# Two-layer graph network on one core: border tiles of the second stage summed once, into a window of 128 nodes that spans two blocks

## The reference

```python
e   = relu(ea @ ee_w1 + ee_b1) @ ee_w2 + ee_b2
agg = segment_sum(x[src] + e, dst, num_segments=n)
h   = (1.0 + eps) * x + agg
h   = relu(_ln(h @ w1 + b1, g1, be1))      # 256 -> 1024
h   = relu(_ln(h @ w2 + b2, g2, be2))      # 1024 -> 1024
out = relu(_ln(x + h @ w3 + b3, bn_g, bn_b))
```

## Time and profile before

| | |
|---|---|
| median of 3 runs | 1556.49 us (1520.37, 1556.49, 1563.42) |
| the profiled execution | 1535.62 us, span 1533.7 us |
| mean granted clock of TensorE | 0.874 of full |
| PE busy | 1254.0 us, 82% of the span |
| DVE busy | 959.9 us, 63% |
| POOL busy | 824.7 us, 54% |
| ACT busy | 678.4 us, 44% |

### The profile page before, as it was taken

One profiled execution on the slowest core, in us unless ns is written; L12 is line 12 of the kernel. 1 busy time (PEld: TensorE's weight loads), 2 busy tenths in 40 slices (PEclk: granted clock), 3 DMA queues, 4 the chain that ended last, 5 costly groups with the idle time before them and its releaser, 6 DMA issues.

```text
span 1533.7 us, 21066 instructions
## 1 busy us (share of the span) xinstructions
PE 1254.0 (82%) x5295; PEld 993.8 (65%) x5295; DVE 959.9 (63%) x2787; ACT 678.4 (44%) x1654; POOL 824.7 (54%) x840
## 2 busy tenths in 40 slices
PE   4888878888879978877877878886888788878997
PEld 3666666666667666766655756665667667656776
DVE  4766666776666776766744655554565556546665
ACT  2455555565555664545332423332443334323443
POOL 6656555666556666654654564443555456544530
PEclk9788889998878989889988988888898889979999
DMA  6435445555455444546654564544555556554530
GB/s 194 114 112 154 140 134 154 159 155 157 141 146 145 133 134 129 157 126 184 186 153 127 154 189 129 148 141 121 158 154 160 153 145 178 156 149 136 161 111 16
DMA packets 106088, 222.13 MB, mean 145 GB/s; under 512 B 20003, under 2 KB 57369, under 8 KB 106010
## 3 DMA queue, kind: packets, MB, share of 16 engines
q0 software_dynamic: 53408, 164.16, 38.3%
q1 hardware_dynamic: 52602, 57.11, 12.1%
HBM read 203.96 MB, written 17.23 MB: 144 GB/s over the span
## 4 chain that ended last, share of the span: by engine, by line
PE 49%; another core or an unknown queue 15%; issue 14%; DVE 10%; ACT 10%; DMA 1%; POOL 0%; DVEq 0%; ACTq 0%; POOLq 0%; SPq 0%
PE ps_z L1307 21%; PE ps_e L1040 8%; PE ps_y L1307 4%; PE ps_sum L1045 4%; PE ps_sum L1047 4%; PE ps_s L1262 3%; ACT msg L1579 3%; DVE msg L2071 2%; DVE msg L2077 2%; ACT msg L1582 2%; ACT aF L1804 2%; PE ps_tr L1376 2%; DVE oh L159 1%; PE ps_w L1141 1%
## 5 line engine op out<-in xcount | busy, mean ns | idle before, releaser
L963 POOL DMA_INDIRECT grow<-table_dram,src_all x401 | 386.0, 963 | 379.5 <-PE ps_s L1262 250.1
L908 POOL DMA_INDIRECT raw<-in_x,src_all x399 | 404.5, 1014 | 257.4 <-DVE msg L2077 143.7
L1307 PE MATMUL ps_z<-w_high,a 128*128 128x512 f32 x784 | 292.3, 441 | 77.3 <-issue 60.5
L2071 DVE SCALAR_TENSOR_TENSOR msg<-raw,w_sb,msg 128x256 fp32r<-128x256 f32 x416 | 183.8, 482 | 212.2 <-ACT msg L1582 139.0
L1040 PE MATMUL ps_e<-we,attr 65*128 65x256 f32 x832 | 254.9, 431 | 47.2 <-DVE msg L2077 36.6
L1045 PE MATMUL ps_sum<-msg,oh 128*128 128x512 f32 x464 | 251.9, 543 | 29.7 <-DVE msg L2077 23.0
L1307 PEld LDWEIGHTS ps_z<-w_high,a 128*128 128x128 f32 x784 | 167.1, 214 | 130.6 <-issue 78.6
L1582 ACT ACTIVATE msg<-ps_e 128x512 fp32r<-128x512 f32 (+1 forms) x220 | 124.1, 564 | 254.3 <-remote 158.9
L1040 PEld LDWEIGHTS ps_e<-we,attr 65*128 65x128 f32 x832 | 175.2, 217 | 94.7 <-issue 62.0
L159 DVE TENSOR_SCALAR oh<-lane,rel 128x128 fp32r<-128x128 f32 x915 | 209.4, 291 | 3.6 <-issue 3.4
L1047 PE MATMUL ps_sum<-msg,oh 128*128 128x512 f32 x464 | 203.0, 437 | 6.3 <-issue 6.2
(11 more groups left out here) (182 smaller groups left out, 1577.8 us busy)
## 6 DMA issues: line engine op xcount, KB each, us to landing
attr<-in_attrT SPq DMA_DIRECT2D x50, 192.0 KB
raw<-in_x,src_all POOLq DMA_INDIRECT x416
grow<-table_dram,src_all POOLq DMA_INDIRECT x401
w_raw<-in_m_w SPq DMA_DIRECT2D x48, 128.0 KB
table_dram<-table SPq DMA_DIRECT2D x23, 256.0 KB
attr<-in_attrT SPq DMA_DIRECT2D x24, 160.0 KB
xs<-in_x SPq DMA_DIRECT2D x24, 128.0 KB
xTb<-in_xT SPq DMA_DIRECT2D x24, 128.0 KB
```

What stands on the lines that cost most here:

```text
L908: pool.indirect_dma_start(out=raw[:, j, :], out_offset=None, in_=x, in_offset=bass.IndirectOffsetOnAxis(ap=src_all[:, q * TILES + j:q * TI ...
L963: pool.indirect_dma_start(out=grow[:, j, :].bitcast(F32), out_offset=None, in_=table_dram, in_offset=bass.IndirectOffsetOnAxis(ap=src_all[ ...
L1307: mm = pe.matmul(acc, left[a], right[b], start=False, stop=stop and a == 1, skip_group_check=True)
L2071: dve.scalar_tensor_tensor(msg[:, j, 1, 0:D], raw[:, j, :], w_sb[:, tile_cols(n, j)], msg[:, j, 0, 0:D].bitcast(F32), ALU.mult, ALU.subtract)
```

## The change

In the program that the inputs select, positions 3 to 24 no longer run step 0 at all, and no longer tile 0 of step 1. A border's two tiles (tile 16 of a block and tile 0 of the block behind) are summed once: their one-hot matrices are made against 128 nodes that begin at node 64 of this block and end at node 63 of the block behind, the window. Each such tile is two matmuls of 256 columns (high part, low part) into columns 256 to 511 of `ps_y`. ACT writes zeros there first (`open_window`). When the sums of a position are done, DVE adds partitions 64 to 127 of the window to h, a third addition in `take_h`, and in the next pass adds partitions 0 to 63 to `hbx` (`carry`), before that position's h is taken. Position 2 makes the first window, positions 0 and 1 stay as they were. The test at the start now asks of the first and last `edge` tiles of a block that their targets lie within 64 nodes of the border. `sum_done` keeps its values: where step 0 is gone, step 1 adds 2. The numbers in `row_free` are unchanged, so tile 16's buffer still waits for the value 10p + 1, which now comes with step 1.

```diff
+LANES, WINDOW = 1, 2
+WINDOWS = 2
+HALF = P // 2
+def has_window(p):
+    return not isinstance(p, int) or p >= WINDOWS
+def behind_window(p):
+    return not isinstance(p, int) or p > WINDOWS
 class Near:
+    def tile_kind(self, p, c, j):
+        span = self.steps[c][0]
+        if behind_window(p) and (c == 0 or span == 0 and j < self.edge):
+            return None
+        if has_window(p) and (span == 1 or span == 0 and j >= TILES - self.edge):
+            return WINDOW
+        return LANES
     def sum_inc(self, p, c):
...
+        if behind_window(p):
+            return c + 1 if c == self.steps_at(p)[0] else 1
# TensorE
+                def add_window_tile(j, slot):
+                    for half in range(2):
+                        mm = pe.matmul(ps_y[:, D:2 * D], oh[:, slot, :], grow[:, j, half * D:(half + 1) * D],
+                                       start=False, stop=False, skip_group_check=True)
+                    return mm
                 def near_step(path, p, c):
...
                     for j in range(j0, j0 + m):
+                        kind = path.tile_kind(p, c, j)
+                        if kind is None:
+                            continue
+                        if kind == WINDOW and (c, j) == path.first_window(p):
+                            pe.wait_ge(window_open, p - WINDOWS + 1)
                         pe.wait_ge(got[j], 16 * path.fills(p + span, j))
-                        mm = add_tile(j, path.slot[c] + j - j0, c == first and j == j0,
-                                      c == last and j == j0 + m - 1)
+                        if kind == LANES:
+                            mm = add_tile(j, path.slot[c] + j - j0, (c, j) == first, (c, j) == last)
+                        else:
+                            mm = add_window_tile(j, path.slot[c] + j - j0)
# ScalarE
+                def open_window(p):
+                    wait(act, carried, p - WINDOWS)
+                    act.activation(ps_y[:, D:2 * D], lane[:, 0:D], ACT.Copy, scale=0.0).then_inc(window_open, 1)
                     if exists(i - 2):
                         finish_std(i - 2, 1)
+                    if exists(i + 1):
+                        open_window(i + 1)
                     if exists(i - 1):
                         deviation(1, i - 1)
# VectorE
+                def make_window_lanes():
+                    dve.wait_ge(oh2_ready, SUMS)
+                    dve.tensor_copy(lane[:, 0:HALF], lane[:, P:P + HALF]).then_inc(window_lanes, 1)
+                    dve.tensor_copy(lane[:, 3 * P:3 * P + HALF], lane[:, 2 * P:2 * P + HALF])
+                    dve.tensor_copy(lane[:, 3 * P + HALF:4 * P], lane[:, P + HALF:2 * P]).then_inc(window_lanes, 1)
                 def take_h(b, steps, loaded, windows=True):
...
+                    if windows and behind_window(b):
+                        dve.wait_ge(carried, b - WINDOWS)
                     dve.tensor_tensor(h[:, :], ps_s[:, 0:D], hbx[:, :], ALU.add).then_inc(h_half, 1)
...
+                    dve.tensor_tensor(h[:, :], ps_s[:, D:2 * D], h[:, :], ALU.add).then_inc(h_summed, 1)
+                    dve.wait_ge(h_summed, b - WINDOWS + 1)
+                    dve.wait_ge(y_done, b - 1)
+                    dve.tensor_tensor(h[HALF:P, :], ps_y[HALF:P, D:2 * D], h[HALF:P, :], ALU.add)\
+                       .then_inc(h_ready, 1)
+                def carry(b):
+                    dve.wait_ge(hb_in, 16 * (b + 1))
+                    dve.tensor_tensor(hbx[0:HALF, :], ps_y[0:HALF, D:2 * D], hbx[0:HALF, :], ALU.add)\
+                       .then_inc(carried, 1)
                     if exists(i):
                         h_low(i)
+                    if exists(i + 1):
+                        carry(i)
                     if exists(i - 2):
                         finish2(i - 2)
```

More of the change, by code:

```diff
@@ L82, in __init__, with steps_at, tiles, first_and_last @@
         self.ahead = [k for k in range(LAST_PAIRS, NP) if PAIRS[k][0] + PAIRS[k][1] <= TILES - edge]
+    def steps_at(self, p):
+        if not behind_window(p):
+            return sum_steps_at(p)
+        return [c for c in range(1, SUMS) if any(self.tile_kind(p, c, j) for j in self.tiles(c))]
+    def tiles(self, c):
+        _, j0, m = self.steps[c]
+        return range(j0, j0 + m)
+    def tile_kind(self, p, c, j):
[5 more added lines that the diff above has]
+        return LANES
+    def first_and_last(self, p):
+        steps = self.steps_at(p)
+        if isinstance(p, int) and p == 1:
+            steps = self.ahead[0:1] + steps
+        plain = [(c, j) for c in steps for j in self.tiles(c) if self.tile_kind(p, c, j) == LANES]
+        return plain[0], plain[-1]
+    def first_window(self, p):
+        return [(c, j) for c in self.steps_at(p) for j in self.tiles(c) if self.tile_kind(p, c, j) == WINDOW][0]
     def sum_inc(self, p, c):
@@ L89, in sum_inc, with one_hot_inc @@
             return 1 + len(self.ahead)
+        if behind_window(p):
+            return c + 1 if c == self.steps_at(p)[0] else 1
         return sum_inc_at(p, c)
+    def one_hot_inc(self, p, steps):
+        if behind_window(p):
+            return steps[-1] + 1 if steps[0] == self.steps_at(p)[0] else len(steps)
+        return sum(sum_inc_at(p, c) for c in steps)
     def one_hots(self, p, c):
@@ L1282, in near_step @@
                     span, j0, m = path.steps[c]
-                    first, last = sum_steps_at(p)[0], sum_steps_at(p)[-1]
-                    if isinstance(p, int) and p == 1:
-                        first = path.ahead[0]
-                    if c == first:
+                    first, last = path.first_and_last(p)
+                    if c == first[0]:
                         wait(pe, h_ready, p)
@@ L1384, in sums @@
                 def sums(path, p, first, end):
-                    for c in sum_steps_at(p):
+                    for c in path.steps_at(p):
                         if first <= c < end:
@@ L1853, in late_iteration @@
                     h_high(i)
+                    if i + 1 == WINDOWS:
+                        act.wait_ge(w_ready, LAYER_2)
+                        act.wait_ge(window_lanes, 2)
+                        open_window(WINDOWS)
                     deviation(1, i - 1)
@@ L2010, in _ @@
                 lim = TILES - edge
[L2011 to L2013 removed]
+                parts = ((slice(0, edge), -HALF, HALF), (slice(edge, lim), 0, P), (slice(lim, TILES), HALF, P + HALF))
+                for part, low, _ in parts:
+                    ins = dve.tensor_scalar(bad[:, n, :, part], rel[:, :, part], float(low), None, ALU.is_lt)
+                ins.then_inc(prep, 1)
                 dve.wait_ge(prep, 6 + 2 * n)
[L2015 to L2018 removed]
+                for part, _, above in parts:
+                    ins = dve.scalar_tensor_tensor(bad[:, n, :, part], rel[:, :, part], float(above),
+                                                   bad[:, n, :, part], ALU.is_ge, ALU.add)
+                ins.then_inc(prep, 1)
                 dve.wait_ge(prep, 7 + 2 * n)
@@ L2326, in near_oh @@
                 def near_oh(path, p, group):
-                    steps = [c for c in range(OH_GROUPS[group][0], OH_GROUPS[group][1] + 1) if c in sum_steps_at(p)]
+                    steps = [c for c in range(OH_GROUPS[group][0], OH_GROUPS[group][1] + 1) if c in path.steps_at(p)]
                     if not steps:
```

37 lines of the change are left out of this document (22 added, 15 removed).

## The result

| | before | changed |
|---|---|---|
| median, us | 1541.41 (4 runs, 1520.37 to 1563.42) | 1668.49 (4 runs, 1662.30 to 1691.08) |
| ratio, 95% interval | | 1.094 (1.086 to 1.102) |
| span of the profiled execution | 1533.7 | 1660.5 |
| PE busy | 1254.0 | 1253.4 |
| mean granted clock | 0.874 | 0.843 |

The account below looks back on a forecast made before the run. It took each pass as bound by a burst of 17 gathers that slows all engines but POOL, then PE's leftover work. Terms of -5.5 + 0.3, about -5 us, took 1546 to 1541 us; range 1515 to 1566.

Parts of the forecast that it names:

- The gather of tile 16: In POOL's list: released later, it delays tiles 0 to 3 by 0.45 us, already counted; not late for its reader, nothing more.
- The 8.5 us: In the loop: part of an average 31.9 us pass that PE needn't work, measured against a pass of 23.4 us.
- rival 1: Loop passes: the stall pattern shifts favourably, -20 us, with the half-clock price of removed matmuls about 1510 us; chance 0.12.
- PE's net of -9.3 us: On PE, positions 2 to 24: 9.9 us of matmuls removed, less 0.6 us for window tiles, at full clock.
- 2.9 us: On PE: the change's saving by the Trainium skill's matmul spacing, set aside because the trace disagreed.
- take_h: On DVE: two one-hots fewer, one 64-partition addition more, upper bound 425 ns taken; together about zero.
- The carry: On DVE: up to 0.425 us before the second stats, hidden in clean passes; 0 to 1.7 us, taken as 0.
- open_window: On ACT: 0.37 us, 23 times, hidden before an instruction waiting for DVE's stats; 8.5 us at most.
- Rival 2: Loop passes: carry and late release slow it, up to 0.88 us a pass; 1565 us, or 1574 at half clock; chance 0.10.
- Rival 3: Loop's back edge: instruction fetches cost 6.1 us in each of 21 passes, +128 us, about 1670 us; chance 0.02.
- The range: For the whole kernel's time: 1515 to 1566 us, leaving out less than 2 in 10.

Follow-up runs that it names:

- e1: The kernel before, with only the release of tile 16's gather moved from step 0 to step 1; 1663.53 us, 1.088 of the kernel before.
- e2: The changed kernel, with tile 4's gather waiting two steps longer (step 4 instead of step 2); 1483.37 us, 0.968 of the kernel before.
- e17: The changed kernel with short pauses before tiles 4, 10 and 16 of every position, and pauses in the first stage; 1413.83 us, 0.933 of the kernel before.
- e18: The kernel before with the same pauses as e17; 1405.60 us, 0.928 of the kernel before.
- e11: The changed kernel with a short pause before tile 7, and before tiles 6 and 12 in the first stage; 1458.02 us, 0.953 of the kernel before.
- e13: e11 with the carry moved behind layer 2's normalization and open_window behind that layer's first relu; 1438.15 us on another chip.
- e14: The kernel before with the pauses of e11 and a dummy DVE instruction of the carry's size in its place; 1405.44 us on another chip.
- e4: The kernel before with a second pause in each burst, before tile 10 until tile 9's gather has landed; 1472.42 us, 0.954 of the kernel before.

## Why the prediction was wrong

**The failed step** is "The gather of tile 16": "all of them start later with it, as just counted ... Cost nothing more". The shift itself was right: from the first sum to the burst's first gather it is 1.72 us now (899.59 to 901.31) and was 1.16 (1070.21 to 1071.37), 0.56 us where 0.45 was said. But I counted it against PE's sums of this pass only, not against the other thing in POOL's queue that waits for the same semaphore. Relative to the burst, step 2 comes 1.0 us earlier (2.5 us behind the first gather for 3.5). That removes the pause of 1.96 us ahead of tile 4, and with it what had kept the stall to the burst's end. e1 has this and nothing else of the change and loses as much; e2 puts a pause back and wins it all.

The row was there to read. In the pass that I quoted as the clean one, POOL stands for 1.96 us behind its fifth gather, and in the pass of 48.3 us ahead of it it does not:

```profile
1031.92 0.95 POOL L963 DMA_INDIRECT grow<-table_dram,src_all  x1 [9.46 <-PE ps_s L1262]
...
1038.37 0.95 POOL L963 DMA_INDIRECT grow<-table_dram,src_all  x1 [0.51 <-issue]
1039.62 0.95 POOL L963 DMA_INDIRECT grow<-table_dram,src_all  x1 [0.30 <-issue]
1041.93 0.95 POOL L963 DMA_INDIRECT grow<-table_dram,src_all  x1 [1.37 <-remote]
```

That burst rests only behind its seventh gather, for 1.37 us, and PE's first gap comes 9.4 us after its start. The whole loop is like that. Of the 21 passes between the two marks of the earlier trace rows, four last over 35 us (38.4, 42.2, 48.3 and 43.4), and they are the four whose burst has no rest of over 1.5 us; in the other 17 bursts POOL rests 1.7 to 2.1 us behind the fifth gather (once 4.2), and PE's first gap comes 9.3 to 14.3 us after that rest. Each of the four is followed by one of the four passes of 23.4 to 23.5 us. So even the clean pass is not free of a stall: that of its own burst sets in at 1089.8, behind the next mark (1087.93). The 8.5 us by which I set it under the average were read off one half of a pair. I had read only POOL's last and first gather of a burst and took its 17 gathers for a constant, in rival 1 too: "Against: burst length and POOL's list are the same". The list was, the timing within it was not. "In which all engines but POOL slow down near the end" should have been asked further: near the end of what, and in which bursts early?

**PE's net of -9.3 us** was sized by rows that hold: 365 matmuls of 512 columns on `ps_s` and 92 of 256 on `ps_y`, as forecast. None of it reached the time. With the bursts freed of stalls (e17, e18) POOL is the bound; the changed kernel is not faster there either, but 7 us slower. By the Trainium skill, in TensorE: Matmul & The Clock Gate, section Back-to-back issue gap, I had set 2.9 us against it; neither sum is borne out, as the term never was on the path.

**take_h.** The upper bound for 64 partitions was the right one: the group of 23 such additions has a mean of 428 ns, the one of 128 partitions 425. PE's matmuls did not wait for h in the changed kernel's loop by any row. **The carry** is 0.41 us (22 times), and e11 shows it in a chain that ends in PE's wait, which "so it is hidden" didn't foresee; what it costs stays open (e13, e14). **open_window** was hidden in the changed kernel: 0.37 us long, and no wait at the window matmuls.

**The rivals.** Rival 1 had the right object (the stall pattern) and the wrong sign; the loss of 127 us is the one it put at -20. Rival 2 named the late release but priced it at its own length, 0.45 to 0.85 us a pass, where the loss is 5.8 (127/22). Rival 3's time, 1670, is hit by accident: fetch packets are 27 and 51 as before, and e1 gives the same time with the lists of the kernel before. Fetching has no part in the loss.

**The range.** It was built from terms that each shift a pass by fractions of a microsecond. The rows said that passes differ by 25 us for a cause that I had not found. A cause unfound of that size belongs in the range, on both sides.

**Still open:** what slows PE and ACT, and DVE with them, at once. It shows in runs of gathers of over some 9 us without a pause of over 1.5 us, in the changed kernel it ends when the last has landed, and its beginning doesn't depend on their bytes or rows; whether it is the count of gathers, POOL's time in them or their queue was not told apart. Nor is it explained why POOL needs some 3 us to go on when it has come to an unfulfilled wait, which is what made the pause: the two matmuls of step 2, begun at 1074.86, were done by about 1075.5, 4.1 us behind the first gather, and tile 4's began at 7.9.

## What to carry to other kernels

Where a queue works in bursts, read one burst gather by gather, with each wait in it, before pricing a change that moves its release: a wait inside may do good by being late. When passes of the same work differ by a factor of two, find what sets them apart before counting instructions; here it was worth over ten times what the change was priced at. A short pass beside a long one is not yet a price: ask first whose wait falls on which side of the mark. A deliberate short wait on a landed gather, so placed that no run exceeds six wherever the burst starts, in the second stage, with like ones in the first, brought both kernels 7% under the one before.

## What the runs showed of the hardware

- After some 9 us of gathers one behind the other, PE has gaps of 0.6 to 4.9 us with no semaphore named, and ACT stands for up to 17.6 us. In the changed kernel PE's first gap comes 8.5 to 9.4 us after the burst's first gather in 20 of 21 bursts (11.0 in the other), and the last gathers have landed before the engines are regular again. Half the bytes or half the rows don't put it off (8.9 and 8.5 us). In runs of five or six gathers (up to 7.8 us, e18 and e4) it doesn't appear. In the kernel before, a rest of 1.96 us starts the count anew; one of some 1.2 us did not keep the gap off (e2: at 9.8 us in such bursts, 2.3 to 3.2 us long).
- A gather of 64 rows takes POOL 0.90 us, one of 128 rows 0.95; rows of 256 or of 512 numbers make no difference (0.95).
- On one chip, executions of the kernel before spread over 1507 to 1587 us, those of e18 over 1402 to 1414 and those of e1 over 1659 to 1673. The spread is wide only where some bursts have the pause and others not, so I put it down to their pattern; that is not shown by itself.
